# First stage of a two-lane macaron block: a four-chunk ring for the position table, the next first normalisation at the head of a phase, and a new order of TensorE and ScalarE within a phase

## The chip, the cores and the metric

One core of one Trainium2 chip runs the whole kernel. The metric is the device time of one execution in microseconds (us), the median of the runs. Below, PE is TensorE, DVE is VectorE, ACT is ScalarE, POOL is GpSimd and SP is SyncE, which here only issues DMAs.

## The reference

The input x is 2 batches of 2048 tokens of width 256. The block is a mixture of experts, an attention with relative positions, and the same mixture again:

```python
x = x + 0.5 * ffn(layernorm(x), Wg, A, B)           # 8 experts of rank 16, top 2
x = x + attn(layernorm(x), Wq, Wk, Wv, Wr, u, v)    # 16 heads of 16
x = x + 0.5 * ffn(layernorm(x), Wg, A, B)

def ffn(x, Wg, A, B):
    gate_logits = xs @ Wg
    topw, sel = top_k(gate_logits, 2); topw = softmax(topw)
    cw = sum(one_hot(sel, 8) * topw[..., None], axis=1)
    h = einsum('td,edr->ter', xs, A)
    return einsum('ter,erd->td', h * cw[..., None], B)

def attn(w, Wq, Wk, Wv, Wr, u_bias, v_bias):
    q, k, v = w @ Wq.T, w @ Wk.T, w @ Wv.T          # split into heads
    rp = r @ Wr.T                                   # r: sines and cosines of 2*L-1 distances
    AC = (q + u_bias) k^T;  BD = rel_shift((q + v_bias) rp^T)
    return softmax((AC + BD) * scale) v
```

## The kernel before, in words

The program has three stages with a barrier between them. The second (attention, some 2,700 us) and the third (the last mixture) are not touched. The change is in the first stage, which makes the first mixture, writes its result to DRAM as `x_one`, normalises it a second time, projects it to q, k and v, and splits q + u, q + v, k and the projected position table each into three bf16 parts that add up to the f32 value.

Tokens go in groups of four tiles of 128. Eight groups are dealt to two lanes, so a lane has four rounds. A lane owns four PSUM banks and one set of buffers; `normed` is one buffer of a lane, used in turn by the first normalisation (of x) and the second (of x_one).

The stage begins with the position table: 8 chunks of 512 positions (`pos_sb`, 512 KB each), 2 items per chunk (`pos_item` L403). An item is 4 matmuls of PE into a bank of lane 1, a copy to `proj` and a first part by ACT (`pos_copy`, `pos_part`), a `rest` by DVE (L567), two parts by POOL (L671, L673) and a store by SP (L374). `proj` has 4 slots, the parts have 6: ACT's copy of item i waits for the `rest` of item i-4, and its first part of item i for the landed store of item i-6. Lane 0's first mixture and the normalisations of both lanes are laid between the items by hand. `pos_sb` holds two chunks; SP issues the load of chunk c+2 once PE has used chunk c, but only after the stores of the earlier items, for each of which it waits (L366 to L375).

Then come eight phases (`PHASES`). Phase (a, b) runs the mixture of lane a's group beside the projection of lane b's, and the next phase swaps the lanes. In this text T1 is the transpose of a's first normalisation (L248, 8 matmul rows in the trace), "hidden" the matmul with the gate and expert weights (L259), T2 the transpose of b's second normalisation (L248 again), then q, k and v (L437, L437, L445), T3 the transpose of `hw` (L266) and "out" the matmul back (L272). PE goes through T1, T2, hidden, q, k, T3, k, out, v. DVE goes through a's gate chain (`logits` to `hw`, L172 to L214), b's six `rest`, a's addition into `x_one_sb` (L224, "the y addition" below), a's second normalisation (`stats`, `var`, `rstd`, `normed`: L136 to L149) and last b's first normalisation of its next round. ACT copies `normed_t` for T1 and T2, takes the `Exp` of the gates (L239), copies and splits the projections, and takes the root of each variance (L158). The order on each engine is written by hand as a list of generators (`order`); nothing is scheduled by a program.

The lines that set it, in the kernel before (DVE, PE, ACT):

```python
if b[1] + 1 < ROUNDS:
    finish(first_norm(b[0], b[1] + 1))
...
for which in (first, second, first, second, second, second, first, second, first, second, second):
...
for which in (first, second, first, second, first, second, first, second):
```

Of the kernel before, what the change touches and what calls it, by code (L numbers as in the profile page):

```python
# [26 lines left out]
P = 128  # L27
# [6 lines left out]
def build_program(nc, x, wq_t, wk_t, wv_t, wr_t, u_bias, v_bias, w_in, w_out, pos_t, ident, fold, iota, out):  # L34
# [5 lines left out]
    KT = D // P  # L40
# [16 lines left out]
    with ctx:  # L57
# [74 lines left out]
        def layer_norm(dve, B, S, base, no, tile, normed):  # L132
# [14 lines left out]
            dve.wait_ge(chain, base + (2 * TG + 1))  # L147
            for t in range(TG):
# [128 lines left out]
        with ExitStack() as c1:  # L277
# [7 lines left out]
            pos_sb = s1("pos_sb", [P, 2, KT, BANK])  # L285
# [23 lines left out]
            pos_loaded = [sem(f"pos_loaded{i}") for i in range(2)]  # L309
# [29 lines left out]
            def _(sp):  # L339
                def load_pos(c):  # L340
                    sp.dma_start(pos_sb[:, c % 2],
                                 pos_t[:, c * BANK:(c + 1) * BANK].rearrange("(k p) n -> p k n", p=P))\
                        .then_inc(pos_loaded[c % 2], 16)
# [10 lines left out]
                load_pos(1)  # L354
                load_x(1)
                for dst, src in ((wq_sb, wq_t), (wk_sb, wk_t), (wv_sb, wv_t)):
# [8 lines left out]
                for c in range(NPC):  # L365
                    if c + 2 < NPC:  # L366
                        sp.wait_ge(pos_projected, (c + 1) * KT)
                        load_pos(c + 2)
                        if c % 2 == 0:
                            load_x(2 + c // 2)  # L370
# [32 lines left out]
            def _(pe):  # L403
                def pos_item(i):

                    c, m = i // KT, i % KT
                    if m == 0:
                        pe.wait_ge(pos_loaded[c % 2], 16 * (c // 2 + 1))
                    if i >= 4:
                        pe.wait_ge(pos_proj_out, i - 3)  # L410
                    for kt in range(KT):
                        last = pe.matmul(PB["bank"][i % 4][:, :], lhsT=wr_sb[:, kt, m * P:(m + 1) * P],
                                         rhs=pos_sb[:, c % 2, kt, :], start=(kt == 0), stop=(kt == KT - 1))
# [37 lines left out]
                def order(first, second):  # L451

                    for which in (first, second, first, second, second, second, first, second, first, second, second):
# [22 lines left out]
            def _(act):  # L476
# [21 lines left out]
                def project(lane, n):  # L498

                    B, S = LB[lane], LS[lane]  # L500
                    for kt in range(KT):
# [8 lines left out]
                    for half in range(2):  # L510
# [3 lines left out]
                        for j in range(2 * KT) if half == 0 else range(2 * KT, NSPLIT):  # L514
                            i = j % KT + (KT if j >= 2 * KT else 0)
# [12 lines left out]
                    if n + 1 < ROUNDS:  # L528
                        root(act, B, S, 2 * n + 3)

                def order(first, second):

                    for which in (first, second, first, second, first, second, first, second):
# [29 lines left out]
            def _(dve):  # L563
# [20 lines left out]
                def first_norm(lane, n):  # L584
# [3 lines left out]
                    yield from layer_norm(dve, LB[lane], LS[lane], n * NSTEP, 2 * n + 1, x_tile(lane, n), LS[lane]["normed"])  # L588
# [26 lines left out]
                def order(a, b):  # L615

                    up, rest = (gates(*a) if a is not None else iter(())), rests(*b)
# [667 lines left out]
```

## Time and profile before

| what | us |
|---|---|
| median of 3 runs (3118.35 to 3139.53) | 3118.8 |
| the profiled execution | 3117.44 |
| its span, first to last instruction | 3115.6 |
| around the span | 1.8 |
| first T1 of the phases starts | 71.29 |
| first q of the phases starts | 75.21 |
| last v of the first stage ends | 279.5 |
| second stage's first instruction | 294.6 |

Busy shares over the span are averages of three different stages: TensorE 92%, VectorE 84%, ScalarE 80%, GpSimd 74%. In the first stage alone they are 50 to 63%, so this stage has to be read by its waits and its order. Times in the rows are microseconds from the start of the span, durations too unless marked ns; what stands in brackets is the idle time of the engine before the row and what ended it. Matmuls in f32 stand as two trace rows each.

### The profile page before, as it was taken

The page shows a single profiled execution, that of the slowest core. Times are in us where ns is not written, and L with a number is a line of the kernel's source. Part 1 is how long each engine was busy: PE and PEld are TensorE (multiplying, and loading weights), DVE is VectorE, ACT ScalarE, POOL GpSimd, SP SyncE. Part 2 cuts the span into 40 slices and gives each one's busy share as a digit, 9 for nine tenths or more (in the row PEclk, how much of TensorE's full clock was granted, in tenths as well). Part 3 has the DMA queues.
Part 4 walks back from the last instruction along what each step waited for, and adds up shares of the span by engine and source line. Part 5 has one row for each costly group of instructions (what it writes and reads, how often), then busy time and mean ns, then how long its engine had stood idle before and what let it go on. Part 6 is the DMA issues. An engine that isn't in the chain of part 4 may idle for free. (4 is left out here: it accounts for less than half of the span.)

```text
span 3115.6 us, 110070 instructions
## 1 busy us (share of the span) xinstructions
PE 2880.4 (92%) x40768; PEld 2031.6 (65%) x40768; DVE 2632.4 (84%) x5042; ACT 2497.8 (80%) x3854; POOL 2310.7 (74%) x4135
## 2 busy tenths in 40 slices
PE   6664799999999999999999999999999999999955
PEld 3452377777777777767776777777776777777644
DVE  4663389999989999978998999999998999999966
ACT  3443689898888888978988888888888889888732
POOL 4443888888888888878888888888788888888800
PEclk8886699999999999999999999999999999999977
DMA  6446888888888888878888888888888888888731
GB/s 202 152 130 164 202 216 230 223 232 230 226 221 225 226 229 224 228 201 224 227 227 225 223 232 222 232 225 227 221 229 224 224 225 227 231 224 222 210 123 55
DMA packets 290276, 657.40 MB, mean 211 GB/s; under 512 B 189520, under 2 KB 256976, under 8 KB 272336
## 3 DMA queue, kind: packets, MB, share of 16 engines
q0 software_dynamic: 190960, 526.89, 64.0%
q1 hardware_dynamic: 98784, 123.38, 13.5%
q8 instruction: 339, 5.55, 0.7%
q14 instruction: 193, 1.58, 0.2%
HBM read 77.19 MB, written 46.14 MB: 40 GB/s over the span
## 5 line engine op out<-in xcount | busy, mean ns | idle before, releaser
L826 POOL DMA_DIRECT2D score<-score x3999 | 2178.3, 548 | 498.4 <-ACT score L1065 428.6
L1063 ACT COPY score<-pos_bank 128x512 f32<-128x512 f32 x2048 | 1104.1, 597 | 280.3 <-PE pos_bank L939 277.6
L1073 ACT ACTIVATE score<-score,low 128x1024 f32<-128x1024 f32 x1024 | 1197.0, 1170 | 34.3 <-DVE low L1126 30.3
L1135 DVE COPY prob_t<-pt_bank 128x512 f32<-128x512 f32 x1792 | 1161.8, 684 | 3.0 <-PE pt_bank L1005 2.9
L1005 PEld LDWEIGHTS pt_bank<-ident_sb,score 128*128 128x128 f32 x8192 | 950.0, 142 | 216.5 <-DVE prob_t L1135 46.2
L1005 PE MATMUL pt_bank<-ident_sb,score 128*128 128x128 f32 x8192 | 1083.6, 275 | 7.7 <-ACT score L1073 5.7
L1126 DVE CUSTOM_DVE_ANT_0 score<-ac_bank,score 128x1024 f32<-128x1024 f32 x512 | 627.1, 1225 | 241.3 <-PE ac_bank L991 116.9
L1126 DVE CUSTOM_DVE_ANT_0 score<-ac_bank,score,low 128x1024 f32<-128x1024 f32 x512 | 657.2, 1284 | 55.8 <-PE ac_bank L991 47.3
L939 PE MATMUL pos_bank<-pos,qv 96*32 96x512 bf16 (+15 forms) x12160 | 658.7, 317 | 29.6 <-DMA qv<-qv_parts 25.3
L1019 PE MATMUL acc_bank<-prob_t,vs 128*32 128x128 f32 x16384 | 662.7, 279 | 3.8 <-issue 3.6
L991 PE MATMUL ac_bank<-ks,qu 96*128 96x512 bf16 x2048 | 622.8, 386 | 25.8 <-DVE low L1126 24.4
L1019 PEld LDWEIGHTS acc_bank<-prob_t,vs 128*32 128x32 f32 x16384 | 385.8, 109 | 177.9 <-issue 174.9
L939 PEld LDWEIGHTS pos_bank<-pos,qv 96*32 96x32 bf16 x12160 | 323.1, 97 | 99.2 <-issue 27.9
L991 PEld LDWEIGHTS ac_bank<-ks,qu 96*128 96x128 bf16 x2048 | 116.5, 97 | 338.1 <-DVE low L1126 227.0
L1081 ACT COPY prob_t<-pt_bank 128x512 f32<-128x512 f32 x256 | 149.8, 585 | 17.7 <-PE pt_bank L1005 17.7
L671 POOL CAST part<-rest 128x512 bf16<-128x512 f32 x64 | 49.1, 767 | 149.6 <-DVE rest L567 149.6
L977 PEld LDWEIGHTS pos_bank<-fold_sb,acc_sb 128*128 128x128 f32 x1024 | 134.6, 192 | 21.5 <-issue 1.7
L977 PE MATMUL pos_bank<-fold_sb,acc_sb 128*128 128x32 f32 x1024 | 125.3, 265 | 2.2 <-issue 1.5
L1088 ACT COPY acc_sb<-acc_bank 128x512 f32<-128x512 f32 x128 | 74.9, 585 | 30.7 <-PE acc_bank L1019 25.6
L248 PE MATMUL bank_one<-ident_sb,normed_one 128*128 128x128 f32 x128 | 26.2, 388 | 68.3 <-DVE normed_one L149 67.5
L673 POOL TENSOR_TENSOR part<-rest,part 128x512 bf16<-128x512 f32 x64 | 83.5, 1304 | 5.1
L1126 DVE DVE_READ_ACCUMULATOR2_ANT low<- 128x1 f32 x1024 | 85.1, 83 | 0.0
(94 smaller groups left out, 867.3 us busy)
## 6 DMA issues: line engine op xcount, KB each, us to landing
score<-score POOLq DMA_DIRECT2D x3937, 129.5 KB, 5.1
pos<-pos_parts SPq DMA_DIRECT2D x96, 128.0 KB, 8.5
qv<-qv_parts SPq DMA_DIRECT2D x192, 64.0 KB, 7.2
ks<-k_parts SPq DMA_DIRECT2D x192, 64.0 KB, 7.1
qu<-qu_parts SPq DMA_DIRECT2D x192, 64.0 KB, 7.2
v_heads<-v_sb SPq DMA_DIRECT2D x8, 1024.0 KB, 6.0
vs<-v_heads SPq DMA_DIRECT2D x32, 256.0 KB, 8.0
pos_parts<-part SPq DMA_DIRECT2D x16, 384.0 KB, 3.7
```

What stands on the lines that cost most here:

```text
L673: pool.tensor_tensor(B["part"][:, slot, 2, :], B["rest"][:, slot, :], B["part"][:, slot, 1, :], ALU.subtract).then_inc(part3, 1)
L826: pool.dma_start(shifted(odd, s, groups, 0), shifted(odd, s, groups, QUAD - 1 - s))\
L939: last = pe.matmul(dst[row:row + QUAD, col + lo:col + hi], lhsT=qv[k // NI % 2][:, q0:q0 + QUAD], rhs=pos[u][:, at + lo:at + hi], start=Tr ...
L977: last = pe.matmul(POS[FOLD_AT % 3][:, f * VW:(f + 1) * VW], lhsT=acc_sb[:, f * P:(f + 1) * P], rhs=fold_sb[:, :], start=True, stop=True)
L991: last = pe.matmul(AC[:, c * BANK:(c + 1) * BANK], lhsT=qu[u][:, i * P:(i + 1) * P], rhs=ks[u][:, first:first + BANK], start=True, stop=True)
L1005: last = pe.matmul(PT[c % 2][:, t * P:(t + 1) * P], lhsT=score[:, slot(k), c * BANK + t * P:c * BANK + (t + 1) * P], rhs=ident_sb[:, :], i ...
L1019: last = pe.matmul(ACC[t * VW:(t + 1) * VW, f * P:(f + 1) * P], lhsT=vs[k // NI % 2][:, 4 * c + t, :], rhs=prob_t[:, c, t * P:(t + 1) * P] ...
L1063: act.copy(score[:, at + f, c * BANK:(c + 1) * BANK], ring(m)[:, :]).then_inc(pos_out, 1)
L1073: act.activation(cols, cols, ACT.Exp, bias=low[:, slot(k), NH - 1:NH], scale=-1.0)\
L1081: act.copy(prob_t[:, c, :], PT[c % 2][:, :]).then_inc(copied_act, 1)
L1126: dve.tensor_tensor_reduce(cols, AC[:, :], cols, SCALE, low[:, slot(k), h - 1:h] if h else -NEG, ALU.add, ALU.min, low[:, slot(k), h:h + 1 ...
L1135: dve.tensor_copy(prob_t[:, c, :], PT[c % 2][:, :]).then_inc(copied, 1)
```

## The change

Three things change in the first stage, and nothing elsewhere.

1. `pos_sb` has four chunks. Chunks 0 to 3 are loaded at the start, chunk c+4 once chunk c is used. DVE's first normalisation no longer waits for the small tables (`iota` and others); that wait stands behind it.
2. On DVE, b's next first normalisation is the first thing in a phase. As it writes lane b's `normed`, it waits for T2 of the same lane (`free`). The second normalisation follows the y addition at once; one `rest` moves behind it.
3. PE: hidden before T2. ACT: the root of the next first normalisation is the first thing in a phase, `Exp` comes before the `normed_t` copies of T2, the copy of `hw_t` between the second and third of q's four parts, and the root of the second normalisation behind the v copies.

```diff
-        def layer_norm(dve, B, S, base, no, tile, normed):
+        def layer_norm(dve, B, S, base, no, tile, normed, free=None):
...
             dve.wait_ge(chain, base + (2 * TG + 1))
+            if free is not None:
+                dve.wait_ge(*free)
...
-            pos_sb = s1("pos_sb", [P, 2, KT, BANK])
+            NPS = 4
+            pos_sb = s1("pos_sb", [P, NPS, KT, BANK])
...
                 load_pos(1)
+                load_pos(2)
                 load_x(1)
+                load_pos(3)
...
                 for c in range(NPC):
-                    if c + 2 < NPC:
+                    if c + NPS < NPC:
                         sp.wait_ge(pos_projected, (c + 1) * KT)
-                        load_pos(c + 2)
-                        if c % 2 == 0:
-                            load_x(2 + c // 2)
+                        load_pos(c + NPS)
+                    if c % 2 == 0 and 2 + c // 2 < len(X_PARTS):
+                        load_x(2 + c // 2)
...
-                    for which in (first, second, first, second, second, second, first, second, first, second, second):
+                    for which in (first, first, second, second, second, second, first, second, first, second, second):
...
                 def project(lane, n):
 
                     B, S = LB[lane], LS[lane]
+                    if n + 1 < ROUNDS:
+                        root(act, B, S, 2 * n + 3)
+                    yield
...
                         for j in range(2 * KT) if half == 0 else range(2 * KT, NSPLIT):
+                            if j == KT:
+                                yield
...
-                    if n + 1 < ROUNDS:
-                        root(act, B, S, 2 * n + 3)
...
-                    for which in (first, second, first, second, first, second, first, second):
+                    for which in (second, first, first, second, second, first, second, second, second, first):
...
-                    yield from layer_norm(dve, LB[lane], LS[lane], n * NSTEP, 2 * n + 1, x_tile(lane, n), LS[lane]["normed"])
+                    yield from layer_norm(dve, LB[lane], LS[lane], n * NSTEP, 2 * n + 1, x_tile(lane, n), LS[lane]["normed"],
+                                          (LS[lane]["norm2_tp"], n * KT) if n else None)
...
                 def order(a, b):
 
+                    if b[1] + 1 < ROUNDS:
+                        finish(first_norm(b[0], b[1] + 1))
...
                     after = second_norm(*a) if a is not None else iter(())
+                    next(after, None)
                     next(rest)
                     next(after, None)
                     next(rest)
-                    next(after, None)
+                    finish(after)
                     finish(rest)
-                    finish(after)
-                    if b[1] + 1 < ROUNDS:
-                        finish(first_norm(b[0], b[1] + 1))
-
-                dve.wait_ge(w_loaded, 16 * 4)
...
                 finish(first_norm(0, 0))
+                dve.wait_ge(w_loaded, 16 * 4)
```

TensorE at the head of the second phase, before. Lane 0 is a (banks 0 to 3), lane 1 is b (banks 4 to 7).

```order
L248 MATMUL bank0_one<-ident_sb,normed_one0 128x128 x4
L248 MATMUL bank1_one<-ident_sb,normed_one0 128x128 x4
L248 MATMUL bank4_one<-ident_sb,normed_one1 128x128 x4
L248 MATMUL bank5_one<-ident_sb,normed_one1 128x128 x4
L259 MATMUL bank2_one<-w_in_sb,normed_t_one0 128x136 x4
L259 MATMUL bank3_one<-w_in_sb,normed_t_one0 128x136 x4
L437 MATMUL bank6_one<-normed_t_one1,wq_sb 128x512 x2
```

The same place after:

```order
L250 MATMUL bank0_one<-ident_sb,normed_one0 128x128 x4
L250 MATMUL bank1_one<-ident_sb,normed_one0 128x128 x4
L261 MATMUL bank2_one<-w_in_sb,normed_t_one0 128x136 x4
L261 MATMUL bank3_one<-w_in_sb,normed_t_one0 128x136 x4
L250 MATMUL bank4_one<-ident_sb,normed_one1 128x128 x4
L250 MATMUL bank5_one<-ident_sb,normed_one1 128x128 x4
L442 MATMUL bank6_one<-normed_t_one1,wq_sb 128x512 x2
```

T2 (banks 4 and 5) has moved behind hidden (banks 2 and 3).

ScalarE from the splits of the first phase to the projection copies of the second, before:

```order
L518 ACTIVATE part0<-proj0 128x512 x2
L158 ACT_TABLE_LOAD
L158 ACTIVATE root_one1<-var_one1 128x4
L525 COPY v_sb0<-bank2_one 128x16x16 x2
L525 COPY v_sb0<-bank3_one 128x16x16 x2
L158 ACTIVATE root_one0<-var_one0 128x4
L236 COPY normed_t_one0<-bank0_one 128x512
L236 COPY normed_t_one0<-bank1_one 128x512
L503 COPY normed_t_one1<-bank4_one 128x512
L503 COPY normed_t_one1<-bank5_one 128x512
L239 ACT_TABLE_LOAD
L239 ACTIVATE ex_one0<-diff_one0 128x4
```

The same stretch after:

```order
L528 ACTIVATE part0<-proj0 128x512 x2
L535 COPY v_sb0<-bank2_one 128x16x16 x2
L535 COPY v_sb0<-bank3_one 128x16x16 x2
L160 ACT_TABLE_LOAD
L160 ACTIVATE root_one1<-var_one1 128x4 x2
L238 COPY normed_t_one0<-bank0_one 128x512
L238 COPY normed_t_one0<-bank1_one 128x512
L241 ACT_TABLE_LOAD
L241 ACTIVATE ex_one0<-diff_one0 128x4
L511 COPY normed_t_one1<-bank4_one 128x512
L511 COPY normed_t_one1<-bank5_one 128x512
```

The table load and both roots now stand behind the v copies, both roots are of the same lane, and the exponential has moved ahead of T2's two copies (L511).

VectorE from the y addition of the first phase on, before:

```order
L224 TENSOR_TENSOR x_one_sb1<-bank7_one,x_all 128x256 x2
L567 SCALAR_TENSOR_TENSOR rest0<-proj0,bias_sb,part0 128x512
L136 BN_STATS stats_one1<-x_one_sb1 128x6 x4
L139 BN_AGGR mean_var_one1<-stats_one1 128x2 x4
L567 SCALAR_TENSOR_TENSOR rest0<-proj0,part0 128x512
L142 TENSOR_SCALAR var_one1<-mean_var_one1 128x4
L567 SCALAR_TENSOR_TENSOR rest0<-proj0,part0 128x512
L145 RECIPROCAL rstd_one1<-root_one1 128x4
L149 TENSOR_SCALAR normed_one1<-x_one_sb1,mean_var_one1,rstd_one1 128x256 x4
L136 BN_STATS stats_one0<-x_all 128x6 x4
L139 BN_AGGR mean_var_one0<-stats_one0 128x2 x4
L142 TENSOR_SCALAR var_one0<-mean_var_one0 128x4
```

The same stretch after:

```order
L226 TENSOR_TENSOR x_one_sb1<-bank7_one,x_all 128x256 x2
L136 BN_STATS stats_one1<-x_one_sb1 128x6 x4
L139 BN_AGGR mean_var_one1<-stats_one1 128x2 x4
L575 SCALAR_TENSOR_TENSOR rest0<-proj0,bias_sb,part0 128x512
L142 TENSOR_SCALAR var_one1<-mean_var_one1 128x4
L575 SCALAR_TENSOR_TENSOR rest0<-proj0,part0 128x512
L145 RECIPROCAL rstd_one1<-root_one1 128x4
L151 TENSOR_SCALAR normed_one1<-x_one_sb1,mean_var_one1,rstd_one1 128x256 x4
L575 SCALAR_TENSOR_TENSOR rest0<-proj0,part0 128x512
L136 BN_STATS stats_one1<-x_all 128x6 x4
L139 BN_AGGR mean_var_one1<-stats_one1 128x2 x4
L142 TENSOR_SCALAR var_one1<-mean_var_one1 128x4
```

The last `rest` of lane 0 stands behind the second normalisation, and what follows is the first normalisation of lane 1, for the phase after next, in place of lane 0's, for the next phase.

## Rows read from the trace of the kernel before

**Rows 1.** The page, busy tenths and granted clock in 40 slices of 78 us.
```profile
PE   6664799999999999999999999999999999999955
...
PEclk8886699999999999999999999999999999999977
```
**Rows 2.** Windows from q to q: PE, PEld, DVE, ACT, POOL busy, clock, DMA.
```profile
75.21:104.23 29.02, 18.97 (x79) 14.08 (x78) 19.07 (x66) 12.98 (x25) 14.64 (x15) 0.82 0.56 182
...
217.68:245.55 27.87, 17.65 (x78) 12.76 (x77) 18.96 (x66) 12.44 (x25) 12.59 (x12) 0.82 0.45 141
245.55:267.18 21.63, 14.62 (x55) 9.30 (x53) 15.49 (x52) 10.29 (x21) 12.46 (x12) 0.84 0.35 118
```
**Rows 3.** Waits of the first 285 us: total, times, longest.
```profile
PE bank_one L248 <- DVE normed_one L149: 67.5, 8, 10.2
...
PE bank_one L412 <- DMA pos_sb<-pos_t: 29.6, 5, 10.5
```
**Rows 4.** Timeline of the position part: start, duration, engine, what.
```profile
12.84 0.37 SPq L341 DMA_DIRECT2D pos_sb<-pos_t  x1
...
24.78 3.70 PE L412 MATMUL bank_one<-pos_sb,wr_sb 128*128 128x512 f32 x8 [1.56 <-DMA pos_sb<-pos_t]
...
28.06 4.87 DVE L567 SCALAR_TENSOR_TENSOR rest<-proj,part 128x512 f32<-128x512 f32 x5
...
34.39 0.49 SPq L341 DMA_DIRECT2D pos_sb<-pos_t  x1
...
39.39 6.67 PE L412 MATMUL bank_one<-pos_sb,wr_sb 128*128 128x512 f32 x8 [10.48 <-DMA pos_sb<-pos_t]
...
47.90 1.42 DVE L224 TENSOR_TENSOR x_one_sb<-bank_one,x_all 128x256 f32<-128x256 f32 x4 [14.96 <-PE bank_one L272]
...
59.49 5.17 PE L412 MATMUL bank_one<-pos_sb,wr_sb 128*128 128x512 f32 x8 [8.27 <-DMA pos_sb<-pos_t]
```
**Rows 5.** DMA issues of the position stores: KB each, us to landing.
```profile
pos_parts<-part SPq DMA_DIRECT2D x16, 384.0 KB, 3.7
```
**Rows 6.** Timeline of VectorE from a y addition on.
```profile
113.53 1.42 DVE L224 TENSOR_TENSOR x_one_sb<-bank_one,x_all 128x256 f32<-128x256 f32 x4 [1.92 <-PE bank_one L272]
...
117.70 1.12 DVE L142 TENSOR_SCALAR var_one<-mean_var_one 128x4 f32<-128x4 f32 x1
...
119.54 3.57 DVE L149 TENSOR_SCALAR normed_one<-x_one_sb,mean_var_one,rstd_one 128x256 f32<-128x256 f32 x4
123.03 1.39 DVE L136 BATCH_NORM_STATS2 stats_one<-x_all 128x6 f32<-128x256 f32 x4
...
125.40 1.38 DVE L149 TENSOR_SCALAR normed_one<-x_all,mean_var_one,rstd_one 128x256 f32<-128x256 f32 x4
132.61 0.26 DVE L172 COPY logits_one<-bank_one 128x16 f32<-128x16 f32 x2 [5.83 <-PE bank_one L259]
```
**Rows 7.** Line L149, window 118 to 123.5: duration ns min/median/max, first and last start.
```profile
L149 DVE TENSOR_SCALAR normed_one<-x_one_sb,mean_var_one,rstd_one x4: 492/1002/1312, 119.5 to 121.8; 128x256 f32<-128x256 f32 x4
```
**Rows 8.** Timeline of TensorE in three phases.
```profile
113.26 3.62 PE L445 MATMUL bank_one<-wv_sb,normed_t_one 128*128 128x256 f32 x16
...
126.93 3.65 PE L248 MATMUL bank_one<-ident_sb,normed_one 128*128 128x128 f32 x16 [10.05 <-DVE normed_one L149]
...
132.41 3.60 PE L437 MATMUL bank_one<-normed_t_one,wq_sb 128*128 128x512 f32 x8
...
186.37 3.19 PE L259 MATMUL bank_one<-w_in_sb,normed_t_one 128*128 128x136 f32 x16
...
267.18 5.42 PE L437 MATMUL bank_one<-normed_t_one,wq_sb 128*128 128x512 f32 x8 [0.68 <-ACT normed_t_one L503]
```
**Rows 9.** Timeline of ScalarE: a table load, a root and the two copies of T2.
```profile
52.95 1.28 ACT L158 ACT_TABLE_LOAD   x1
54.24 0.21 ACT L158 ACTIVATE root_one<-var_one 128x4 f32<-128x4 f32 x1
...
73.08 1.09 ACT L503 COPY normed_t_one<-bank_one 128x512 f32<-128x512 f32 x2
```

More of the change, by code:

```diff
@@ L308, in build_program @@
             w_proj_loaded, wr_loaded = sem("w_proj_loaded"), sem("wr_loaded")
-            pos_loaded = [sem(f"pos_loaded{i}") for i in range(2)]
+            pos_loaded = [sem(f"pos_loaded{i}") for i in range(NPS)]
             pos_projected, pos_proj_out = sem("pos_projected"), sem("pos_proj_out")
@@ L340, in load_pos @@
                 def load_pos(c):
-                    sp.dma_start(pos_sb[:, c % 2],
+                    sp.dma_start(pos_sb[:, c % NPS],
                                  pos_t[:, c * BANK:(c + 1) * BANK].rearrange("(k p) n -> p k n", p=P))\
-                        .then_inc(pos_loaded[c % 2], 16)
+                        .then_inc(pos_loaded[c % NPS], 16)
                 def load_x(i):
@@ L407, in pos_item @@
                     if m == 0:
-                        pe.wait_ge(pos_loaded[c % 2], 16 * (c // 2 + 1))
+                        pe.wait_ge(pos_loaded[c % NPS], 16 * (c // NPS + 1))
                     if i >= 4:
@@ L412, in pos_item @@
                         last = pe.matmul(PB["bank"][i % 4][:, :], lhsT=wr_sb[:, kt, m * P:(m + 1) * P],
-                                         rhs=pos_sb[:, c % 2, kt, :], start=(kt == 0), stop=(kt == KT - 1))
+                                         rhs=pos_sb[:, c % NPS, kt, :], start=(kt == 0), stop=(kt == KT - 1))
                     last.then_inc(pos_projected, 1)
```

## The prediction

> **What bounds the kernel now.** I read the page by slices first [rows 1]. A slice is 78 us; PE is below nine tenths, and its granted clock below full, only in the first five slices and the last two. The change touches the first stage alone, which is over at 294.6, so 2,820 of 3,115.6 us stay as they are. A measurement of this kernel can tell about 1%, 31 us, from no change, and the stage that is changed is 295 us long: for that the stage would have to move by a tenth.
>
> Next the windows, cut from one q matmul to the next [rows 2]. Of a phase of 27.9 us PE is busy 17.7, DVE 19.0, ACT 12.4, POOL 12.6: no engine bounds it, a chain does. The six q starts from 75.21 to 217.68 are five intervals, together 142.5 us, 28.5 each; the next two are 27.9 and 21.6. The waits name the chain [rows 3]: PE waits 67.5 us for `normed` at the heads of the phases, and 29.6 us in five waits for chunks of the position table.
>
> One phase in order of time, counted from its y addition [rows 6]: the y addition at 113.53, the second normalisation over at 119.54 + 3.57 = 123.1 (9.6 later), the first normalisation of the next group over at 126.8, then T1 and T2 at 126.93, hidden, and q at 132.41 [rows 8]. From q to the next y addition it is 9.3 (104.23 to 113.53) [rows 2, 6]. So a phase is 9.3 + 9.6 + 9.3 = 28.2.
>
> **Part 1, the position ring.** What goes: chunk 4 was asked for at 34.39, behind SP's waits for stores, and PE took it at 39.39 after 10.5 us of idleness, at the low clock (6.67 for eight rows, 3.60 to 3.70 at the high one) [rows 4]. With the ring it is asked for where chunk 2 was, about 12.84. PE then starts chunk 4 when T3 is done, about 28.2, and "out" is over at 34. The y addition, 47.90 before, comes then: 13.9 earlier. Had nothing else been late, all of that would reach the phases.
>
> What is late next is the store ring, and DVE. The first part of item 8 waits for the landed store of item 2, whose `rest` DVE makes only behind lane 0's gate chain, at 28.06 [rows 4]. POOL takes about 2.3 us an item there and a store lands 3.7 us after issue [rows 5]: item 2 at 34.7, item 3 at 37.3, item 4 at about 41.5, because 1.5 MB of chunk 6 and x go out ahead of it. So ACT ends item 10's part at 42.1 and the root of lane 0's second normalisation comes at 43.6, behind a table load of 1.28 [rows 9] (54.24 before). From there DVE is the chain: normalisation 1.4, two `rest` 1.7, statistics 1.7, one `rest` 0.7, `var` 0.7, the next normalisation 2.6 with POOL busy, five more `rest` 4.4 (they take 4.87 with POOL busy [rows 4]): 57.2. Then the first normalisation of (0,1) comes before anything of the phase: statistics 1.7 and `var` 0.9, root at 60.0. Two copies 1.05, hidden at the low clock 3.05 (3.19 with its drain [rows 8]), T2 1.75 (half of the 3.65 of T1 and T2 together, less drain), normalisation 1.4, gates 1.0, root and `Exp` 0.2, two copies 1.1 [rows 9]: the first q at 69.8, before 75.21. The term is **-5.4**. Its bounds: -1 (if every store lands as late as the slowest, and DVE's `rest` all take 1 us) and -12 (the 13.9 less 2).
>
> **Part 2, one phase in the new order.** The start of q is Q.
> - Q to the y addition: 9.3 as before, since q, k, T3, k and out stand as they did, and the copy of `hw_t` comes sooner.
> - The root of the second normalisation now stands behind the v copies. v ends 12.5 after Q (it starts where the y addition does, less 0.3, and takes 3.6 with its drain [rows 6, 8]), the last copies at 13.2, the table load at 14.4, the root at 14.6, which is 5.3 after the y addition. DVE has statistics, one `rest`, `var` and another `rest` done at 4.6, so it waits 0.8, a wait that did not exist. Then the four operations of `normed`. With POOL busy all the time they took 3.57, the median one 1.00; with POOL idle, on x, four take 1.38 [rows 6, 7]. Here POOL has work for half of that time (its last `rest` is held back), so I take 2 x 1.0 + 2 x 0.35 = 2.7. The end is at 8.3 after the y addition, 9.6 before: 1.3 are won.
> - From there to the next q, all in a row: `rest` 0.7, then statistics, `var` and root 2.2 (with the reciprocal they were 2.37, 123.03 to 125.40, and `var` beside POOL can be 1.12 [rows 6]), two copies of T1 1.05 (T1 itself ran long before), hidden at the low clock 3.05, T2 at the low clock 1.75, first normalisation 1.45, `logits` to `diff` 0.95, `Exp` 0.2, two copies of T2 1.1. Together 12.45, before 9.3. The reason is in the three orders: hidden waits for ACT, ACT waits for the root of a normalisation that only the phase after next wants; T2 waits for hidden, that normalisation waits for T2, the gates for it, `Exp` for the gates, and T2's copies, which q wants, for `Exp`. Two pairs of steps that ran side by side (T2 beside T1's copies, T2's copies beside hidden) now run in a row.
> - The clock. Before, PE ran T1, T2 and hidden without a gap into q, and q had the high clock: 3.60 [rows 8]. Now PE has 4.8 us of work at the low clock, stands for 3.7 us, then starts q. The three rows where eight such rows began at the low clock took 6.67, 5.17 and 5.42 [rows 4, 8]: 3.07, 1.57 and 1.82 over 3.60. I take the mean, **2.2** a phase, bounds 0 and 3.1.
>
> A phase is then 9.3 + 2.2 + 8.3 + 12.45 = 32.3 against 28.5: +3.8, and five intervals give **+19.0**.
>
> The seventh phase has no first normalisation to make. T1's copies go as soon as the root of the second normalisation is there (5.5 to 6.6 after the y addition), hidden to 9.7, `diff` 10.6, `Exp` 10.9, T2's copies to 12.1. The interval is 9.3 + 2.2 + 12.1 = 23.6 against 27.9 [rows 2]: **-4.2**. The eighth has only T2: 9.3 + 8.3 + 1.7 + 0.7 = 20.0, with 0.5 for the clock 20.5 against 21.6: **-1.1**. Behind the last q nothing changes: the end of the stage is POOL's last parts and their stores.
>
> The extra wait of DVE (`free`) has the gates queued behind it, and PE's T3 waits for these. Before, `logits` began 0.2 behind q [rows 6, 8] and T3 was not held; now they begin 2.3 ahead of q, so nothing more is lost there. The loads of x are asked for as early as before, or earlier.
>
> Sum: -5.4 + 19.0 - 4.2 - 1.1 = +8.3 on the profiled execution's 3117.44: 3125.7. The median of the runs, 3118.8, is 1.4 above that execution; I say 3126.
>
> A page that speaks against the change is the Trainium skill's "ScalarE: Activation LUTs", section "What ACT_TABLE_LOAD costs": a switch of table set is said to cost 1283 ns for the load and about 1380 ns of drain. The trace has the load at 1.28, and the root starts 0.01 after its end, at 54.24 [rows 9]. The load used to lie in a wait and now lies between the v copies and a root that DVE waits for. With the page's 1.38 on top, an estimate from that page, seven phases would add 9.7.
>
> **The rivals.**
> - A, only the gains: q keeps the high clock in spite of the gap. For it: a gap of 1.56 us in the position part did no harm (3.70 for the eight rows) [rows 4]. Against: the burst ahead of the gap is itself at the low clock. The sum is 8.3 - 6 x 2.2 = -4.9, 3112.5. With a position part at its better bound it is -11.5, 3106.
> - B, the load's tail is real: something like 1.4 us more between the v copies and the root in each of seven phases, +9.7, 3135.4. For it: the root's end is on the chain now. Against: rows 9.
> - C, clearly faster: hidden is done before the second normalisation ends, as the new order of PE seems to want. Then each of six phases is like my seventh without its clock loss, 21.4, 7.1 below 28.5: -43 - 5 - 1, about 3069. Against: the order of ACT, where the root stands ahead of T1's copies. It decides at whether `normed_t` of T1 is copied before or after that root.
> - D, clearly slower: PE, broken up by the new gap, is at 1.2 GHz from q through out. These 8.9 us double in six phases: 6 x (8.9 - 2.2) = 40 on top of 8.3, 3166. It decides at whether the clock rises before out. Against: in every phase of before it rose within 6.2 us of the start of a long burst, at the latest behind the 3.19 of [rows 8]; and here a burst of 12.5 us follows.
>
> **How the numbers follow.** The forecast has 0.60, A 0.26, B 0.07, C 0.03, D 0.04. A, the forecast and B all lie within 31 us: within 1% is 0.93, faster by over 1% is C's 0.03, slower is D's 0.04. The range takes in A with the better bound of the position part (3106) and, above, a clock loss of 3.1 in six phases (+5.4), `var` at its worst in five (+3.8) and a position part at -1 (+4.4), together 3139: 3104 to 3141.
>
> **What would show it.** Right: the first q near 70; the first y addition near 34; no wait of PE for `pos_sb` after chunk 1; q-to-q intervals of 31 to 34 in five phases, then 23 to 25 and 20 to 21; a gap of PE of 3 to 4 us between T2 and q, with the first q rows near 590 ns each at the high clock and about 800 to 1200 at the low one; a wait of DVE for the root of 0.5 to 1 us. Wrong: q intervals at or below 28, hidden standing ahead of the end of the second normalisation, or a first stage that ends 30 us later or earlier; a second stage whose length differs by more than 5 us would be outside this working altogether.

## The result and the profile after

The changed kernel is slower by 0.39%: ratio 1.0039, 95% interval 1.0021 to 1.0057. Its median is 3138.7 us over 11 runs, that of the kernel before 3127.4 over 11 runs of the same comparison (the 3118.8 ahead was a median of three). As a difference the interval is 6.6 to 17.8 us; the forecast was +8.3. The forecast took 1% as what such a comparison can tell from no change; with this many runs the interval is 0.2% to either side, so 0.39% stands clear of it. The profiled execution has a span of 3136.8, 21.2 more than before.

The q starts of the two traces, which split the first stage into its terms:

| | first q | q to q, seven intervals | last v ends |
|---|---|---|---|
| before | 75.21 | 29.0, 28.2, 27.8, 29.2, 28.3, 27.9, 21.6 | 279.5 |
| after | 71.19 | 33.7, 31.5, 33.5, 34.0, 31.6, 24.6, 20.7 | 293.4 |

So 13.9 of the 21.2 us are in the first stage. From the first matmul of the second stage to the first of the third it is 2727.3 before and 2733.3 after; over the traces of all kernels below, in which that code is the same, it goes from 2727 to 2758 with no relation to the length of the first stage. The rest of the 21.2 us is thus mostly this scatter (6.0 us) and not the change. The prediction had said that a second stage whose length differs by more than 5 us would be outside its working; it differs by 6.0. It is also why each kernel below is judged twice: by the ratio, and by the marks in its trace.

The windows from q to q, the answer to [rows 2] (PE, PEld, DVE, ACT, POOL busy, granted clock, DMA share, GB/s):

```profile
136.35:169.82 33.47, 21.87 (x76) 14.92 (x76) 17.85 (x66) 12.63 (x24) 11.74 (x12) 0.75 0.36 118
235.34:259.89 24.55, 21.19 (x76) 14.24 (x76) 14.49 (x52) 12.42 (x23) 11.75 (x12) 0.82 0.25 85
259.89:280.57 20.68, 14.72 (x52) 9.48 (x53) 12.47 (x32) 10.19 (x19) 11.74 (x12) 0.86 0.58 185
```

Against the window of 217.68 in [rows 2], VectorE's and GpSimd's busy time fell by about 1 us, TensorE's rose from 17.7 to 21.9 at the same instructions, and the granted clock of the phase fell from 0.82 to 0.75.

The waits of the first 300 us, the answer to [rows 3]:

```profile
PE bank_one L261 <- ACT normed_t_one L238: 42.5, 7, 7.2
...
ACT ex_one L241 <- DVE diff_one L183: 40.8, 7, 6.6
ACT root_one L160 <- DVE var_one L142: 38.2, 7, 5.7
DVE normed_one L151 <- PE bank_one L250: 36.2, 6, 6.4
...
PE bank_one L442 <- ACT normed_t_one L511: 23.4, 8, 3.6
...
DVE rstd_one L145 <- ACT root_one L160: 17.2, 16, 6.3
...
PE bank_one L417 <- DMA pos_sb<-pos_t: 11.5, 3, 7.0
```

The 67.5 us in which PE waited for `normed` are gone. In their place PE waits for T1's copies (42.5) and T2's (23.4), ACT for `var` and for `diff`, and DVE for T2: each of them about once a phase, and each released by the one before it. This is one ring of waits, read from five rows.

One phase in order of time, from its y addition, the answer to [rows 6, 8, 9]. VectorE:

```profile
148.47 1.42 DVE L226 TENSOR_TENSOR x_one_sb<-bank_one,x_all 128x256 f32<-128x256 f32 x4 [0.68 <-PE bank_one L274]
...
154.05 0.18 DVE L145 RECIPROCAL rstd_one<-root_one 128x4 f32<-128x4 f32 x1 [1.03 <-ACT root_one L160]
154.26 2.78 DVE L151 TENSOR_SCALAR normed_one<-x_one_sb,mean_var_one,rstd_one 128x256 f32<-128x256 f32 x4
156.97 0.68 DVE L575 SCALAR_TENSOR_TENSOR rest<-proj,part 128x512 f32<-128x512 f32 x1
157.57 1.39 DVE L136 BATCH_NORM_STATS2 stats_one<-x_all 128x6 f32<-128x256 f32 x4
...
166.35 1.38 DVE L151 TENSOR_SCALAR normed_one<-x_all,mean_var_one,rstd_one 128x256 f32<-128x256 f32 x4 [6.26 <-PE bank_one L250]
```

ScalarE:

```profile
152.52 1.28 ACT L160 ACT_TABLE_LOAD   x1
153.81 0.20 ACT L160 ACTIVATE root_one<-var_one 128x4 f32<-128x4 f32 x1
159.68 0.20 ACT L160 ACTIVATE root_one<-var_one 128x4 f32<-128x4 f32 x1 [5.66 <-DVE var_one L142]
159.79 1.05 ACT L238 COPY normed_t_one<-bank_one 128x512 f32<-128x512 f32 x2
...
168.60 0.20 ACT L241 ACTIVATE ex_one<-diff_one 128x4 f32<-128x4 f32 x1 [6.46 <-DVE diff_one L183]
168.72 1.05 ACT L511 COPY normed_t_one<-bank_one 128x512 f32<-128x512 f32 x2
```

TensorE:

```profile
152.60 1.07 PE L250 MATMUL bank_one<-ident_sb,normed_one 128*128 128x128 f32 x8 [0.78 <-issue]
160.90 4.00 PE L261 MATMUL bank_one<-w_in_sb,normed_t_one 128*128 128x136 f32 x16 [7.23 <-ACT normed_t_one L238]
164.69 1.55 PE L250 MATMUL bank_one<-ident_sb,normed_one 128*128 128x128 f32 x8
169.82 6.74 PE L442 MATMUL bank_one<-normed_t_one,wq_sb 128*128 128x512 f32 x8 [3.58 <-ACT normed_t_one L511]
```

T1 is over at 153.7 and its copies wait until 159.8, behind a root that no matmul needs before the T1 of the next phase, at 186.4. Hidden at 160.9, T2 at 164.7, the first normalisation at 166.4 (it had its reciprocal since 160.1), `diff`, `Exp` at 168.6, T2's copies, q at 169.8. From the end of the second normalisation (157.0) to q it is 12.8 us, before 9.3. Then q's eight rows take 6.74, before 3.60.

The position part, the answer to [rows 4]:

```profile
34.21 1.42 DVE L226 TENSOR_TENSOR x_one_sb<-bank_one,x_all 128x256 f32<-128x256 f32 x4 [1.65 <-PE bank_one L274]
...
43.43 0.63 ACT L494 ACTIVATE part<-proj 128x512 bf16<-128x512 f32 x1 [4.50 <-DMA pos_parts<-part]
...
45.38 0.20 ACT L160 ACTIVATE root_one<-var_one 128x4 f32<-128x4 f32 x1
```

PE's two waits for the table behind chunk 1, chunk 6 and chunk 7:

```profile
39.32 3.70 PE L417 MATMUL bank_one<-pos_sb,wr_sb 128*128 128x512 f32 x8 [1.78 <-DMA pos_sb<-pos_t]
...
45.75 5.40 PE L417 MATMUL bank_one<-pos_sb,wr_sb 128*128 128x512 f32 x8 [2.73 <-DMA pos_sb<-pos_t]
```

The y addition is at 34.2 (forecast "about 34"), 13.7 earlier; the first part of item 10 waited 4.5 us for the landed store of item 4, and the root behind it came at 45.4, 8.9 earlier; the first q is only 4.0 earlier.

### The profile page after: what moved, and what is told of

Read it like the earlier page. It is cut to its first block and busy times, and to the rows that moved or that the text cites. A ratio compares the mean times of both kernels' runs of the same rounds, so it can differ in the third digit from the quotient of the medians.

```text
span 3136.8 us, 110076 instructions
## 1 busy us (share of the span) xinstructions
PE 2901.8 (93%) x40768; PEld 2040.3 (65%) x40768; DVE 2625.9 (84%) x5042; ACT 2501.1 (80%) x3854; POOL 2312.0 (74%) x4135
## 5 line engine op out<-in xcount | busy, mean ns | idle before, releaser
L1135 DVE CUSTOM_DVE_ANT_0 score<-ac_bank,score,low 128x1024 f32<-128x1024 f32 x512 | 657.0, 1283 | 56.6 <-PE ac_bank L1000 48.0
L948 PE MATMUL pos_bank<-pos,qv 96*32 96x512 bf16 (+15 forms) x12160 | 660.4, 317 | 32.8 <-DMA qv<-qv_parts 25.9
L682 POOL TENSOR_TENSOR part<-rest,part 128x512 bf16<-128x512 f32 x64 | 76.3, 1192 | 5.1
L575 DVE SCALAR_TENSOR_TENSOR rest<-proj,bias_sb,part 128x512 f32<-128x512 f32 x32 | 29.8, 958 | 52.5 <-ACT part L528 52.5
```

The lines of the kernel that those rows point to most:

```text
L682: pool.tensor_tensor(B["part"][:, slot, 2, :], B["rest"][:, slot, :], B["part"][:, slot, 1, :], ALU.subtract).then_inc(part3, 1)
L948: last = pe.matmul(dst[row:row + QUAD, col + lo:col + hi], lhsT=qv[k // NI % 2][:, q0:q0 + QUAD], rhs=pos[u][:, at + lo:at + hi], start=Tr ...
L1135: dve.tensor_tensor_reduce(cols, AC[:, :], cols, SCALE, low[:, slot(k), h - 1:h] if h else -NEG, ALU.add, ALU.min, low[:, slot(k), h:h + 1 ...
```

## The experiments

Each kernel was timed against the kernel before, with 5 to 12 runs of its own. Times of the form "first q" and "last v" and the intervals are read from one profiled execution each.

**e1: the ring alone.** The kernel before with part 1 of the change.

```diff
-            pos_sb = s1("pos_sb", [P, 2, KT, BANK])
+            NPS = 4
+            pos_sb = s1("pos_sb", [P, NPS, KT, BANK])
...
                 load_pos(1)
+                load_pos(2)
                 load_x(1)
+                load_pos(3)
...
-                dve.wait_ge(w_loaded, 16 * 4)
...
                 finish(first_norm(0, 0))
+                dve.wait_ge(w_loaded, 16 * 4)
```

> The kernel before with the four-chunk ring and the moved wait for the small tables, phases untouched. My theory (the position part wins time, the new order of the phases loses more): without the first normalisation of (0,1) ahead of the first phase and with T1, T2 and hidden together, the first q starts at 61 to 63 (before 75.2, changed kernel 71.2), the seven q-to-q intervals stay at 27.8 to 29.2 and 21.6, so the whole is 12 to 14 us faster than before, ratio near 0.996. Rival (store ring and DVE take the gain back also here): first q at 70 or later, ratio 0.998 to 1.000. Rival (the earlier stores and loads crowd later DMAs): intervals grow by 1 us or more.

Ratio 0.9960 (0.9946 to 0.9975). The first q is at 60.37, 14.8 earlier; the intervals are 29.8, 27.9, 29.3, 28.3, 27.8, 29.3 and 21.6, together 2.2 longer than before; the last v ends at 267.6, 11.9 earlier. The first q of this trace:

```profile
60.37 3.60 PE L440 MATMUL bank_one<-normed_t_one,wq_sb 128*128 128x512 f32 x8
```

The y addition of the position part is at 33.4 here, 14.6 earlier than in the kernel before, so in the old order of the phases all of it reaches the first q. The first rival (the gain taken back) falls. The second (longer intervals) falls on average, at 0.3 us an interval, but not one by one: three intervals grew by 0.8 to 1.6 us, one shrank by 0.9, and 29.8 and the two of 29.3 are above the 27.8 to 29.2 that I had expected.

**e2: the order alone.** The changed kernel with two chunks.

```diff
-            NPS = 4
+            NPS = 2
...
                 load_pos(1)
-                load_pos(2)
                 load_x(1)
-                load_pos(3)
```

> The changed kernel with a two-chunk ring again, so only the new order of the phases. My theory: the intervals are those of the changed kernel (31.5 to 34.0 in five, then 24.6 and 20.7), the first q at 83 to 87, because the position part ends as late as before and the first normalisation, hidden, T2 and Exp then come in a row; 25 to 30 us slower than before, ratio near 1.009. Rival (the phases lose only because the position part leaves them crowded DMAs or a bad start): intervals near 28.5 and a ratio near 1.003.

Ratio 1.0074 (1.0058 to 1.0091). The first q is at 83.03, the intervals 33.8, 31.5, 33.5, 34.0, 31.6, 24.6 and 20.7, those of the changed kernel to 0.1 us. The first q of this trace:

```profile
83.03 6.61 PE L440 MATMUL bank_one<-normed_t_one,wq_sb 128*128 128x512 f32 x8 [3.58 <-ACT normed_t_one L509]
```

So the phases are slow by their own order, wherever they start, and the new order also costs at the first q: +7.8 without the ring (83.03 against 75.21), +10.8 with it (71.19 against 60.37). The ratio is a little better than the 1.009 that I had expected: about 23 us, in place of 25 to 30.

**e3: T2's copies ahead of Exp.** The changed kernel; `first` is ScalarE's list of the mixture (T1's copies, Exp, copy of `hw_t`, root), `second` that of the projection (root, T2's copies, splits, v copies).

```diff
-                    for which in (second, first, first, second, second, first, second, second, second, first):
+                    for which in (second, first, second, first, second, first, second, second, second, first):
```

> The changed kernel, with ScalarE's two copies of T2 ahead of Exp in a phase. My theory (q waits for Exp by order alone, and the gap costs the clock): q starts some 0.6 us behind T2, the first normalisation, logits and Exp lie beside q, first q rows at the high clock for most of their length; five intervals of 27 to 28.5, first q near 67; the whole 14 to 22 us faster than before, ratio near 0.994. Rival (DVE's order is what holds the phase: hw comes late, T3 waits for it): q early but a gap ahead of T3 of 2 us or more, intervals above 30.

Ratio 0.9936 (0.9919 to 0.9952). First q at 67.03, five intervals of 27.2 to 27.3, then 19.9 and 20.7.

The timeline of TensorE in one phase of e3:

```profile
116.03 3.85 PE L261 MATMUL bank_one<-w_in_sb,normed_t_one 128*128 128x136 f32 x16 [7.21 <-ACT normed_t_one L238]
119.72 1.04 PE L250 MATMUL bank_one<-ident_sb,normed_one 128*128 128x128 f32 x8
121.48 3.70 PE L442 MATMUL bank_one<-normed_t_one,wq_sb 128*128 128x512 f32 x8 [0.73 <-ACT normed_t_one L511]
```

That of ScalarE beside it:

```profile
120.36 1.07 ACT L511 COPY normed_t_one<-bank_one 128x512 f32<-128x512 f32 x2 [4.38 <-PE bank_one L250]
...
123.12 0.20 ACT L241 ACTIVATE ex_one<-diff_one 128x4 f32<-128x4 f32 x1 [0.39 <-DVE diff_one L183]
```

q stands 0.7 us behind T2, `Exp` runs beside it, and q has the high clock. Swapping two entries of a list takes 5.6 us from each of the five intervals (32.8 to 27.3) and makes a kernel that is slower than before into one that is faster. Of the 5.6, about 2.9 is the gap (3.58 to 0.73) and 2.3 the clock in q's rows (6.0 on average in these five phases, to 3.70); the remaining 0.4 was not taken apart. The rival is out: T3 has no wait in any phase.

**e4: T1's copies ahead of the root.** The changed kernel.

```diff
-                    for which in (second, first, first, second, second, first, second, second, second, first):
+                    for which in (first, second, first, second, second, first, second, second, second, first):
```

> The changed kernel, with ScalarE's two copies of T1 ahead of the root of the next first normalisation (it stands behind them), Exp still ahead of T2's copies. My theory (hidden waits for that root by order alone): hidden runs beside the second normalisation, 5 us earlier in a phase, T2 at once behind the normalisation; five intervals of 25.5 to 27.5, first q near 67; the whole 18 to 28 us faster than before, ratio near 0.993. Rival (hidden is held by T1 or by banks, not by the root): no change against the changed kernel, ratio near 1.004.

Ratio 0.9948 (0.9932 to 0.9964); first q at 68.37, intervals 26.9 to 27.3 in five, then 24.6 and 20.7. The intervals are as expected, the first q is 1.4 later than the 67 expected, and the whole gains 16 us and not 18 or more. The rival (hidden held by T1 or by banks) is out. The timeline of TensorE in one phase of e4:

```profile
141.01 3.60 PE L261 MATMUL bank_one<-w_in_sb,normed_t_one 128*128 128x136 f32 x16 [1.37 <-ACT normed_t_one L238]
144.41 1.27 PE L250 MATMUL bank_one<-ident_sb,normed_one 128*128 128x128 f32 x8
149.60 6.42 PE L442 MATMUL bank_one<-normed_t_one,wq_sb 128*128 128x512 f32 x8 [3.92 <-ACT normed_t_one L511]
```

Hidden now waits 1.4 us in place of 7.2, but the gap ahead of q (3.9) and the low clock in it are still there. The place of the root and the place of Exp are two separate losses.

**e5: both.**

```diff
-                    for which in (second, first, first, second, second, first, second, second, second, first):
+                    for which in (first, second, second, first, second, first, second, second, second, first):
```

> The changed kernel with both repairs on ScalarE: T1's copies ahead of the root, T2's copies ahead of Exp. My theory: a phase is 9.3 from q to the y addition, 8.5 to the end of the second normalisation, then T2, the root and its two copies: q some 3.5 later; five intervals of 21.5 to 24, first q near 65; the whole 35 to 50 us faster than before, ratio 0.984 to 0.989, faster by over 1%. Rival (something else ends last once these two are gone, such as hw ahead of T3, or POOL's parts): intervals stay above 25 and a wait for that stands in the profile, ratio 0.991 or more.

Ratio 0.9856 (0.9832 to 0.9880): faster by over 1%. First q at 65.25, five intervals of 21.8 to 24.9, mean 22.9; the 24.9 is above the 24 that I had expected at most. T2 and q of one phase in e5's timeline, and q of the next:

```profile
129.20 1.09 PE L250 MATMUL bank_one<-ident_sb,normed_one 128*128 128x128 f32 x8
133.00 6.75 PE L442 MATMUL bank_one<-normed_t_one,wq_sb 128*128 128x512 f32 x8 [2.71 <-ACT normed_t_one L511]
...
157.90 3.70 PE L442 MATMUL bank_one<-normed_t_one,wq_sb 128*128 128x512 f32 x8 [2.71 <-ACT normed_t_one L511]
```

The sum of e3 and e4 would be 5.6 + 5.7, about 11.2 off each interval of 32.8; it is 9.9. The root, one place ahead of T2's copies, keeps a gap of 2.7 us ahead of q in four phases. In three of them the clock fell, and q took 5.4 to 6.8; in the fourth, at 157.90, it did not fall, and q took 3.70. This is what spreads the intervals.

**e6: the gap filled.** The changed kernel with TensorE work in the gap, overwritten by q.

```diff
+                    if n + 1 < ROUNDS:
+                        for _ in range(4):
+                            pe.matmul(B["bank"][2][:, 0:D], lhsT=wq_sb[:, 0, 0:P], rhs=wq_sb[:, 0, :],
+                                      start=True, stop=True)
                     yield
                     pe.wait_ge(S["norm2_t"], n * KT + KT)
```

> The changed kernel with four matmuls added on TensorE behind T2 in the first six phases (wq by wq into q's bank, overwritten by q), to fill the 3.6 us in which it stands before q. Clock theory (the gap costs 1.5 to 3 us a phase at q): the eight q rows take 3.6 to 4.5 in place of 5.1 to 6.7, q starts as before or up to 0.5 later, intervals shorter by 1.5 to 2.5, the whole 8 to 14 us faster than the changed kernel, ratio to before near 1.000. Rival (the low clock at q comes from the whole idle time before hidden, not from this gap): q rows as slow as before or slower by the added work, ratio 1.004 or more.

Ratio 0.9997 (0.9981 to 1.0014), 0.4% below the changed kernel. Intervals 30.3 to 30.7 in five, 2.3 less than the changed kernel on average, and all of one length; the sixth is 21.9 (24.6). The first q is at 69.8, 1.4 earlier than in the changed kernel and not as late or later; the root of the position part was already 0.9 earlier in this trace, so most of this is not the added work's. Hidden, T2, the added work (L439) and q in e6's timeline:

```profile
121.95 3.99 PE L261 MATMUL bank_one<-w_in_sb,normed_t_one 128*128 128x136 f32 x16 [7.20 <-ACT normed_t_one L238]
125.74 1.35 PE L250 MATMUL bank_one<-ident_sb,normed_one 128*128 128x128 f32 x8
126.92 1.89 PE L439 MATMUL bank_one<-wq_sb 128*128 128x256 f32 x8
130.67 3.70 PE L446 MATMUL bank_one<-normed_t_one,wq_sb 128*128 128x512 f32 x8 [1.86 <-ACT normed_t_one L515]
```

The added work was done at the high clock in 1.9 us, the gap left was 1.9, and all six q in front of a gap took 3.70. The clock term is thus measured by itself: the q rows of the changed kernel took 6.57, 5.09, 6.41, 6.74, 5.13 and 6.41, 2.4 over 3.70 on average, and 2.3 in the five phases whose intervals became 2.3 shorter. What decides is the time without TensorE work between T2 and q, not the idle time ahead of hidden, which stayed at 7.2.

**e7: T2's copies ahead of the root too.** On top of e5.

```diff
                 def project(lane, n):
 
                     B, S = LB[lane], LS[lane]
-                    if n + 1 < ROUNDS:
-                        root(act, B, S, 2 * n + 3)
-                    yield
                     for kt in range(KT):
                         act.wait_ge(S["norm2_tp"], n * KT + (kt + 1))
                         act.copy(B["norm_t"][:, kt, :], B["bank"][kt][:, :]).then_inc(S["norm2_t"], 1)
                     yield
+                    if n + 1 < ROUNDS:
+                        root(act, B, S, 2 * n + 3)
+                    yield
```

> Both repairs, and also T2's two copies ahead of the root of the next first normalisation on ScalarE (e5 still showed q waiting 2.7 us for them). My theory: q starts 0.7 us behind T2 and at the high clock; then DVE's chain of root, first normalisation and gates ends last, and T3 waits about 1 us for hw: five intervals of 20.8 to 21.8 (e5: 22.5 on average), the whole 4 to 8 us faster than e5, ratio to before near 0.984. Rival (T3's wait eats all of it): intervals at 22.5 or above and the same ratio as e5.

Ratio 0.9827 (0.9803 to 0.9851). First q at 64.6, intervals 21.0, 21.0, 21.1, 22.6, 20.1, 21.1 and 20.7; last v at 225.1, against 236.2 in e5. T2, q and T3 of one phase in e7's timeline, and hidden of the phase with the 22.6:

```profile
104.83 1.09 PE L250 MATMUL bank_one<-ident_sb,normed_one 128*128 128x128 f32 x8
106.66 3.70 PE L442 MATMUL bank_one<-normed_t_one,wq_sb 128*128 128x512 f32 x8 [0.73 <-ACT normed_t_one L508]
...
113.05 0.66 PE L268 MATMUL bank_one<-ident_sb,hw_one 128*128 128x128 f32 x4 [0.97 <-DVE hw_one L216]
...
144.87 3.56 PE L261 MATMUL bank_one<-w_in_sb,normed_t_one 128*128 128x136 f32 x16 [1.37 <-ACT normed_t_one L238]
```

As forecast: q 0.7 us behind T2, and T3 waits 1.0 us for `hw`, in five of the first six phases. The mean of the five intervals is 21.2, inside the expected 20.8 to 21.8, but two single ones are not: in the phase of the 22.6 hidden ran at the low clock for most of its length (3.56 us, elsewhere 2.12), its T3 found `hw` ready, and the interval after it was 20.1. So the wait for `hw`, at the end of VectorE's chain from the second normalisation over the first to the gates, is worth about 0.9 us of a phase. It is not the only wait left (hidden still waits 1.4 for T1's copies), and no run took it away. The rival falls by the trace. By the time alone e7 can't be told from e5: the two intervals of the ratio overlap.

**e8: x later.** The changed kernel.

```diff
-                    if c % 2 == 0 and 2 + c // 2 < len(X_PARTS):
-                        load_x(2 + c // 2)
+                    if c == 0:
+                        load_x(2)
                     for m in range(KT):
...
+                load_x(3)
+                load_x(4)
```

> The changed kernel, with the last two loads of x (1 MB each) asked for behind the stores of the position table. Store-ring theory (the root at 45.4 comes late because the store of item 4 stands behind 1.5 MB of loads): ScalarE's wait for that store, 4.5 us in the changed kernel, falls to 1 to 2, the root comes at 42 to 43.5 and the first q at 68 to 69.5 in place of 71.2; intervals unchanged; the whole 1.5 to 3 us faster than the changed kernel, too little for the timing, to be read in the trace. Rival (the store is late for its own sake or DVE is the limit): first q at 70.5 to 71.5.

The timeline of ScalarE in the position part of e8, the first part of item 10 and the root behind it:

```profile
40.22 0.63 ACT L496 ACTIVATE part<-proj 128x512 bf16<-128x512 f32 x1 [1.88 <-DMA pos_parts<-part]
...
42.16 0.20 ACT L160 ACTIVATE root_one<-var_one 128x4 f32<-128x4 f32 x1
```

The wait for the store of item 4 fell from 4.5 to 1.9, the root from 45.4 to 42.2, the first q from 71.2 to 68.7: the store did stand behind the loads. The intervals of five phases are 31.5 to 34.0, as in the changed kernel; the sixth is 22.1 (24.6), and why stays open. The ratio, 1.0050 (1.0033 to 1.0066), shows nothing of it: it overlaps with the changed kernel's 1.0039. The last v of this trace ends 4.5 us earlier, and its second stage is 2758.1 long, the longest of all. That the late loads of x do not themselves lengthen the second stage is not shown by this run; in e9, which has them too, it is 2734.1.

**e9: e7 with x later.** The edits of e7 and e8 together.

> The reordering of e7 and the late loads of x together, as the version meant to be best. If both theories hold and add up: first q near 62, intervals as in e7, last v near 227, ratio to before 0.982 to 0.984. Rival (the late loads of x make the first normalisations of the third and later rounds wait): an interval above 24 with a wait of DVE for x, ratio no better than e7.

Ratio 0.9823 (0.9804 to 0.9842), first q at 62.0, last v at 222.3 (e7: 64.6 and 225.1), no wait for x in any interval; the last v is earlier than the 227 expected. The trace shows the 2.6 us at the first q, the timing can't tell them. This is the best version that was run: 1.8% faster than the kernel before, with a last v 57 us earlier.

Not run by itself: the order of PE (hidden before T2), the place of the second normalisation and of the one `rest` on VectorE, and the place of the copy of `hw_t`. So it is shown which places on ScalarE cost, but not which of the other moves makes the repaired order (intervals of 21.2 in e7) shorter than the old one (28.5).

## Why the prediction was right, point by point

- **The whole.** The median of 3138.7 lies within 3104 to 3141, by 2.3 only. Of the 12.7 us above 3126, 8.6 come from the kernel before, which read 3127.4 here and 3118.8 in the three runs that the forecast started from; that the sum stayed inside is in part luck. The fair measure is the difference: +0.39%, about 12 us, against +8.3.
- **The position part, -5.4.** Measured -4.0. The reading was right in its parts: the y addition at 34, the landing of item 4's store as what is late next (e8), DVE's `rest` behind it. The step that missed is that landing: item 10's part ended at 44.1 and not at 42.1, so the root came at 45.4 and not at 43.6. From that root to the root of (0,1) it is 16.0 (forecast 16.4), from there to the first q 9.8 (forecast 9.8). (The steps listed in these two stretches add up to 0.4 and 0.25 less than the times given with them; a root and a reciprocal of 0.2 each are not in the list.) One statement was wrong: PE did wait for `pos_sb` after chunk 1, 1.8 us for chunk 6 and 2.7 us for chunk 7, because SP asked for these loads only behind stores for which it waits. Those waits lay beside DVE's chain.
- **What the ring is worth.** The forecast read -5.4 as the ring's term. e1 and e2 show that it was the sum of two: the ring alone makes the first q 14.8 earlier, and the new order in the first phase gives 10.8 of it back. The working had both inside it, the 13.9 and the steps from 57.2 to 69.8, but not apart, so it did not say that of the change as it stood only the ring was worth keeping (e1, 0.9960). Once three places on ScalarE are mended, the new order adds 1.3% to that (e7, 0.9827), more than the ring itself.
- **One phase, +3.8, five times +19.0.** Measured 32.8 against 28.5, +4.3, in five +21.7. On average over the five, q to the y addition takes 11.7 (forecast 9.3 + 2.2), from there to the end of the second normalisation 8.55 (forecast 8.3; DVE waited 1.0 for the root, forecast 0.8), from there to q 12.1 to 12.95, mean 12.6 (forecast 12.45). The clock term, counted over 3.60 as in the forecast, is 2.4 in these five phases and 2.5 in all six (forecast 2.2). Single phases lie from 1.5 to 3.1, as far apart as the three rows from which it was taken (1.57 to 3.07).
- **The seventh and eighth phase, -4.2 and -1.1.** Measured -3.3 and -0.9 (24.6 and 20.7, forecast 23.6 and 20.5).
- **The sum.** +13.4 at the last q against +8.3. The terms missed by 0.2 to 2.7, all in the same direction; the largest is the phase, where 0.5 us (0.25 up to the end of the second normalisation, 0.2 in the clock, 0.1 behind the normalisation) counts five times.
- **The extra wait of DVE** showed up as 36.2 us of waiting. T3 never waited for `hw` in the changed kernel, as forecast. But the wait is not free there: the first normalisation has its reciprocal at 160.1 and stands until T2 at 166.4, and the gates, `Exp` and T2's copies, for which q waits, are behind it. The forecast had these steps in its 12.45. Only with T2's copies ahead of `Exp` (e3) does q no longer stand behind this wait.
- **Rival A** (q keeps the high clock) is out: q had the low clock in all six phases. **Rival D** is out: the clock was back by k each time. **Rival C** described a kernel that the change was not. e4 is its condition alone, hidden beside the second normalisation: worth 5.7 us a phase, 27.2 and not the 21.4 that the rival gave it, since T2's copies still stand behind `Exp`. Intervals of 21.2 came with e7, in which neither `Exp` nor the root stands ahead of T2's copies any more. **Rival B**, the tail of a table load, is out: v copies over at 152.50, load at 152.52, 1.28 long, root at 153.81, 0.01 behind it, and the same in all seven phases. The Trainium skill, in "ScalarE: Activation LUTs", section "What ACT_TABLE_LOAD costs", states the same 1283 ns for the load and about 1380 ns of drain on top; of the drain the trace shows nothing where the load lies on the path.

## What to carry to other kernels

When instructions on several in-order engines are re-ordered at once, write down for each moved wait what is queued behind it on its engine, and follow that around all engines until it closes: here an early root held T1's copies, and Exp held T2's, and two list entries decided between 0.4% slower and 1.4% faster (1.7% with a third place, e7). These sizes are of this kernel. Put what the next matmul needs ahead of what only a later phase needs. And test a bundle of edits apart: here the ring gained and the order, as written, lost, and inside the order two places made the loss.

## What was not expected of the hardware

- **The clock rose and fell again within one phase.** Between hidden and q, in four windows of the changed kernel (PE, PEld, DVE, ACT, POOL busy, granted clock, DMA):

```profile
128.10:131.60 3.50, 3.50 (x15) 3.50 (x16) 0.00 (x0) 1.21 (x1) 0.00 (x0) 0.50 1.04 285
...
131.70:132.70 1.00, 1.00 (x10) 0.83 (x8) 0.00 (x0) 0.00 (x0) 0.00 (x0) 1.00 1.05 292
...
133.00:136.30 3.30, 0.00 (x0) 0.00 (x0) 3.09 (x24) 1.17 (x3) 0.00 (x0) 0.81 0.38 128
...
136.40:139.00 2.60, 2.60 (x3) 1.13 (x4) 1.49 (x8) 0.00 (x0) 0.00 (x0) 0.50 0.01 3
```

  Hidden ran at 1.2 GHz, T2 at 2.4, and after the 3.58 us of idleness q ran at 1.2 again. The mean of 0.81 in the gap says that it fell while PE stood still, before q. The high clock was reached and lost again before the long matmuls began. Over the runs, counting gaps behind T2 that ran at the high clock or rose to it: of 0.7 to 1.9 us (e3, e5, e6, e7) the clock was kept each time, of 2.71 us (e5) it was lost in three of four, of 3.6 to 4.8 us (changed kernel, e4) each time.
- **Adding TensorE work made the kernel faster.** Four matmuls a phase whose result is thrown away took 0.4% off the changed kernel (0.9981 to 1.0014 against 1.0021 to 1.0057).
- **The second stage scatters more than the terms argued about here.** With the same code it took 2727 to 2758 us over the eleven traces, so a gain of 3 us in the first stage can be seen in a trace and not in the time. What makes the second stage scatter was not tried and stays open.
